# First layer of a two-layer transformer kernel: key and query splits one step earlier, value projections and products shifted by a step

## The reference

```
def _L0_attn_ref(x, Wq, Wk, Wv):            # H = 8 heads, R = 64, d = 128
    Q = (x @ Wq.T).reshape(b, n, H, R)
    K = (x @ Wk.T).reshape(b, n, H, R)
    V = (x @ Wv.T).reshape(b, n, H, d)
    attn = softmax(einsum('bnhr,bmhr->bhnm', Q, K), axis=-1)
    return einsum('bhnm,bmhd->bnd', attn, V)
...
xn = _layernorm(x)
x = x + _L0_attn_ref(xn, ...) + _L0_ffn_ref(xn, ...)   # ffn: 8 experts, top 1, capacity 80
xn = _layernorm(x)
x = x + _L1_attn_ref(xn, ...) + _L1_ffn_ref(xn, ...)   # pairwise attention; 8 experts, top 2
```

## Time and profile before

| | us |
|---|---|
| median of 3 runs | 1464.59 (1461.4 to 1467.53) |
| the profiled execution | 1470.05 |
| its span in the trace | 1468.3 |
| PE busy | 1227.4 (84%) |
| DVE busy | 1235.5 (84%) |
| ACT busy | 1135.5 (77%) |
| POOL busy | 879.0 (60%) |

### The profile page before, as it was taken

How to read it: one execution, slowest core, us unless ns; L and a number is a source line. 1 busy time by engine, 2 the same in 40 slices (tenths; PEclk the granted TensorE clock), 3 DMA queues, 4 the chain that set the end, 5 groups by cost and what they waited for, 6 DMA issues and landing times.

```text
span 1468.3 us, 24950 instructions
## 1 busy us (share of the span) xinstructions
PE 1227.4 (84%) x6185; PEld 586.6 (40%) x6185; DVE 1235.5 (84%) x3409; ACT 1135.5 (77%) x1292; POOL 879.0 (60%) x1294
## 2 busy tenths in 40 slices
PE   3799878888664889988899888998989988899887
PEld 2477556556551233333333333333333333333333
DVE  4665777777665899999999999999999999999997
ACT  1665766666425999989998899988999889998860
POOL 1563632222100587778877788877887878877730
PEclk9999999999966899999999999999999999999998
DMA  5001100000000000000000000000000000000001
GB/s 183 7 11 21 24 7 0 0 0 1 1 19 0 15 19 19 29 25 18 18 18 26 23 23 18 18 23 24 25 18 18 21 25 25 18 18 21 25 26 33
DMA packets 38786, 31.66 MB, mean 22 GB/s; under 512 B 6150, under 2 KB 35609, under 8 KB 38738
## 3 DMA queue, kind: packets, MB, share of 16 engines
q1 hardware_dynamic: 37714, 29.76, 7.0%
q0 software_dynamic: 1024, 1.35, 0.6%
HBM read 29.10 MB, written 2.75 MB: 22 GB/s over the span
## 4 chain that ended last, share of the span: by engine, by line
DVE 30%; PE 27%; issue 9%; DVEq 3%; ACT 1%; POOL 0%; ACTq 0%
DVE arena L1051 18%; PE ps L1331 9%; PE ps L1344 7%; DVE arena L1037 6%; PE ps L1388 4%; PE ps L1408 2%; PE ps L1380 2%; DVE x L1094 2%; PE ps L1362 2%; DVE z L1077 1%; DVE spread L1103 1%; DVE nmax L1043 1%; DVEq L1050 1%; DVEq L1094 1%; ACT arena L1188 1%
## 5 line engine op out<-in xcount | busy, mean ns | idle before, releaser
L1051 DVE SCALAR_TENSOR_TENSOR arena<-arena,ps 128x512 f32<-128x512 f32 x1024 | 662.3, 678 | 65.1 <-PE ps L1344 64.8
L1188 ACT ACTIVATE arena<-arena,eps 128x4096 f32<-128x4096 f32 x128 | 474.1, 3708 | 38.7 <-POOL arena L1311 38.2
L1305 POOL TENSOR_SCALAR arena<-kT,negq 128x512 f32<-128x512 f32 x480 | 331.5, 702 | 193.8 <-DVE arena L1051 178.3
L1344 PE MATMUL ps<-spread,sel 128*128 128x512 f16 x1024 | 348.5, 386 | 118.1 <-DVE arena L1051 111.8
L1311 POOL TENSOR_SCALAR arena<-arena,q 128x512 f32<-128x512 f32 x480 | 350.9, 741 | 22.4
L1344 PEld LDWEIGHTS ps<-spread,sel 128*128 128x128 f16 x1024 | 92.2, 97 | 511.8 <-DVE arena L1051 436.1
L1331 PE MATMUL ps<-arena,phi_cols 128*32 128x512 f32 x2048 | 274.6, 610 | 20.5 <-ACT arena L1188 20.5
L1176 ACT ACTIVATE arena<-kT,q 128x512 f32 (+1 forms) x330 | 217.1, 712 | 3.1
L462 POOL TENSOR_SCALAR kT<-kT,region 128x512 f32<-128x512 f32 x128 | 88.6, 692 | 211.3 <-DVE region L587 211.1
L512 ACT ACTIVATE kT<-ps,region 128x512 f32<-128x512 f32 x128 | 87.9, 686 | 110.2 <-DVE region L582 108.7
L582 DVE TENSOR_REDUCE region<-ps 128x1 f32<-128x512 f32 x128 | 88.3, 690 | 83.5 <-PE ps L687 82.0
(11 more groups left out here) (196 smaller groups left out, 1743.0 us busy)
## 6 DMA issues: line engine op xcount, KB each, us to landing
wge<-in_e_wg SPq DMA_DIRECT2D x32, 256.0 KB, 2.7
w1e<-in_e_w SPq DMA_DIRECT2D x32, 128.0 KB, 2.1
w2e<-in_e_w SPq DMA_DIRECT2D x32, 128.0 KB, 2.1
w3e<-in_e_w SPq DMA_DIRECT2D x32, 128.0 KB, 2.1
region<-in_w SPq DMA_DIRECT2D x1, 2048.0 KB
out<-x SPq DMA_DIRECT2D x4, 256.0 KB, 2.8
region<-in_wqk SPq DMA_DIRECT2D x1, 512.0 KB, 4.7
region<-in_wv SPq DMA_DIRECT2D x1, 512.0 KB, 5.4
```

What stands on the lines that cost most here:

```text
L1051: dve.scalar_tensor_tensor(feat[:, j, k, :], feat[:, j, k, :], 1.0, psB[:, k % BANKS, :], ALU.mult, ALU.mult, accum_out=sums[:, j, gg, c:c ...
L1188: act.activation(grp, grp, ACT.Sqrt, bias=eps[:]).then_inc(e_ready, 2)
L1305: pool.tensor_scalar(feat[:, j, QUADS * gg + c, :], kT[:, b * N:(b + 1) * N], HUGE, negq[:, b % 2, at - b * N // 2:at - b * N // 2 + 1], A ...
L1344: pe.matmul(psB[:, k % BANKS, :], sel[:, gg, c, :], spread[:, j, :], start=True, stop=True).then_inc(bc_done, 1)
```

## The change

```diff
@@ -385,12 +385,12 @@
-        VALUES_AT = {1: 0, 3: 2, 5: 4, 7: 6, 10: 1, 11: 3, 13: 5, 15: 7}
+        VALUES_AT = {2: 0, 3: 2, 6: 4, 7: 6, 10: 1, 11: 3, 14: 5, 15: 7}
         VALUES = list(VALUES_AT.values())
-        QK_AT, Q_HI, K_HI, Q_LO, K_LO = 0, 1, 2, 2, 3
-        STAGE_AT = H * TB - 6
+        QK_AT, Q_HI, K_HI, Q_LO, K_LO = 0, 0, 1, 1, 2
+        STAGE_AT = H * TB - 7
         LAG_T, LAG_LO = 3, 4
-        AV_AT = (8, 9, 10, 10)
+        AV_AT = (8, 9, 9, 10)
```

## The result

The changed kernel takes 1415.32 us (median of 3, 1415.14 to 1419.44) where the kernel before takes 1464.59; the ratio is 0.967, with a 95% interval of 0.963 to 0.972. The profiled execution took 1419.44 us. A second set on another chip gave 1412.9 us (5 runs) against 1464.96, ratio 0.9646 (0.9619 to 0.9673). The forecast was 1414.

A forecast was written before the change was run, and what follows sets the result against it. PE bounds the first layer, waiting 47.2 us for k_lo. Plain heads 22.7 and value heads 19.5 make 42.2 us, the clock 8: 1464.59 - 50.2 gives 1414 us, range 1403 to 1440 (1407 to 1422 at 0.50).

The forecast's parts named there:

- What bounds it: PE in the first layer, held by 47.2 us in 28 waits of the score matmul for k_lo at head starts.
- Plain heads, 9.78 to 8.03: Heads 4 to 7 of a row, without value projections: 1.75 us saved each, 22.7 us over 13 ends.
- Value heads, 10.62 to 9.23: Heads 0 to 3 of a row, two value projections each: wait gone, 19.5 us over 15 ends.
- a sign of a wrong schedule: In the first layer: value heads over 9.5 us, or score waits over 1 us at plain ends.
- Values, products, copy of the row: nothing: Moved value projections, value products and next row's input copy (step 26 to 25): no direct cost, PE's work unchanged.
- The clock, 8 of 11 us: PE's granted clock in the first layer: five of seven low stretches after k_lo waits go, 8 of 11 us.
- The sum: Whole kernel: 42.2 us on PE's path plus 8 of clock, 50.2 us off, giving 1414 us.
- 1 (all waits go, 58 us): PE in the first layer: all 47.2 us of waits and 11 us of clock go, 1406 us; chance 0.13.
- 2 (clock): PE's clock still falls, from several small pauses: 1422 us if as often, 1432 after every plain head; chance 0.16.
- 3 (DVE): DVE at 90% becomes the bound at plain head ends: 33 us saved, 1431 us; chance 0.13.
- 4 (slower, through ACT's queue): ACT's queue in steps 0 and 1 delays PE through pT_lo: 5 to 15 us slower, 1470 to 1480; chance 0.04.
- 5: It does nothing: step 0's scores wait for exp of step 2 or a bank, 1460 to 1465 us; chance 0.04.

The follow-up runs named there:

- experiment 1: The changed kernel's query and key splits alone (1415.85 us) and its value and product moves alone (1473.38 us), otherwise as the kernel before.
- values_only: Value projections and products as in the changed kernel, queries and keys split as before: 1473.38 us, ratio 1.0065 to the kernel before.
- experiment 4: The changed kernel with one, two or three idle copies on DVE ahead of k_lo in plain heads: 1420.17, 1433.85 and 1447.27 us.
- one idle copy: The changed kernel with one idle copy (0.6 us) on DVE ahead of k_lo in plain heads: 1420.17 us.
- experiment 3: ACT's k_hi copies put behind pT_hi: in the changed kernel 1408.66 us, in the kernel with only values and products moved 1457.89 us.

## Why the prediction was right, point by point

The mechanism and the steps came out as set up. That the median was met to within 1 to 2 us is in part luck: in the profiled executions the layer gained 5 us more than forecast, and that does not show in the medians.

- **What bounds it.** Right. The time followed the 47.2 us of waits for k_lo, and moving PE's own work by itself gained nothing (experiment 1, `values_only`).
- **Plain heads, 9.78 to 8.03.** Measured 8.16, so 1.62 saved and not 1.75, for 13 ends at most 21 us in place of 22.7. The chain was the one I set up; one distance was short: the k_hi pair starts 0.80 after exp (182.83 against an exp at 182.03), not the 0.68 that q_hi has in the earlier trace rows. The wait of the transposes was 0.40 (0.37 expected). Their waits add to 7.5 us, in the stated 3 to 8.
- **Value heads, 10.62 to 9.23.** Measured 8.94 to 8.97 in most: 1.65 saved and not 1.39. The wait went as said, and 0.25 more went with it. A PE that has not stopped does step 3 and step 0 in 1.35 + 2.85 = 4.20, and I had 1.92 + 2.55 = 4.47 from a PE that stopped between them. 15 ends give some 4 us more. The third value head lasts 9.9 from the second row on, over the 9.5 that was named as a sign of a wrong schedule; but it was 10.9 before, of which 0.9 was wait, and little more than the wait went. The sign was set without looking at that head.
- **Values, products, copy of the row: nothing.** Right to within 3 us (the layer is 294.7 us with the splits alone and 291.8 with all). But the reason was incomplete: I held the end of a head to be fixed by k_lo's step, and the products' place to be free. With the splits late the same move costs 0.66 us in each plain head. It was free here only because the step that copies k_hi moved ahead of the added products as well.
- **The clock, 8 of 11 us.** All falls went, and they were eight. By the lengths of heads with and without one, six cost 1.6 us each and the last 0.7; the one at 107 us cost nothing, as its head, full of the experts' work, lasts 17.3 us before and after. That is 10.5 us. The mechanism holds (experiment 4); the size was 2.5 us short.
- **The sum.** 50.2 us expected: 42.2 from the waits and 8 from the clock. The layer gave 55.7, of which 10.5 the clock and so 45 the steps, less 0.7 at its end; the second layer, which I had at nothing, took 4.2 back in the profiled execution. Medians: 49.3 and 52.
- **The rivals.** 1 (all waits go, 58 us): the 0.2 of L686 and the 7.5 of L702 stay, so it fell; but by its size the layer's 55 lies nearer to it than to the 50.2. Its reason, that 0.14 is less than a semaphore's delay, isn't in the rows, where the delay from k_lo's end to the scores is that same 0.14 (199.36 + 0.69 to 200.19). 2 (clock): fell, the granted clock stayed at 1.00. The Trainium skill (TensorE: Matmul & The Clock Gate, "A second HAM failure mode: psum-queue depth-cycling") tells of a clock that swings where PE pauses often and shortly between groups of matmuls. Here it did not swing with a pause of 0.4 us a plain head, nor with 0.4 and 0.6 (one idle copy); with 0.4 and 1.2 it fell at four of 13 places. 3 (DVE): fell, DVE is busy 44.43 of 50 us at 204 to 254 us, 89% over heads of both kinds (90% was worked out for plain heads), and keeps up. 4 (slower, through ACT's queue): the mechanism exists, but costs 0.45 us in a plain head and nothing in a value head (experiment 3). 5 fell.

## What to carry to other kernels

When one engine waits for one operand, measure the distance from the first operation of the chain that makes it, not from the last: two edits that look alike, work moved ahead of that chain and the chain moved ahead of the work, differ by 58 us here (1473.38 and 1415.85). Look in each queue for what stands ahead of the chain's links: swapping two operations on an engine with time to spare was worth 0.45 us in each of 13 places. And where a wait goes, add what it did to the clock: the falls were a fifth of what the layer gained (10.5 of 55.7 us).

## What the runs showed of the hardware

- In the runs with idle copies the granted clock of PE fell at none of 13 plain ends with 0.6 us of wait for k_lo (and 0.4 for pT_lo), at four with 1.2 and at five with 1.8; with a single wait of 2.1 (the kernel before) at seven. A fall made a step of 2.56 us one of 4.2, with a granted clock of 0.58 to 0.60 over 4 us.
- The same matmuls took less time where PE did not stop: 4.20 against 4.47 us (its recorded wait taken off) for two steps, the last of a value head and the first of the next head, without any change of clock (1.00 in both). The cause wasn't looked for.
- After an exponential with its sum, ACT starts the next copy 0.68 us later when it is q_hi and 0.80 later when it is the k_hi pair (204.13 to 204.81 in the earlier trace rows, 182.03 to 182.83 after). The cause wasn't looked for.
